# A macaron transformer layer on one core: zero rows by ScalarE, maxima split by VectorE, row loads and stack loads in another order

## The reference

```
quantise(W)  = clip(round(W / (mean|W| + 1e-5)), -1, 1)
ffn(u)       = relu(u @ quantise(W1).T + b1) @ quantise(W2).T + b2      # 128 -> 512 -> 128
attn(u)      = softmax(rope(q) @ rope(k).T / sqrt(8)) @ v, 16 heads of 8 channels, then @ Wo.T + bo
x = x + 0.5 * ffn(layernorm(x))
x = x + attn(layernorm(x))
x = x + 0.5 * ffn(layernorm(x))
```

## Time and profile before

| | us |
|---|---|
| median of 3 executions | 541.2 (540.09 to 543.0) |
| profiled execution, its time | 541.95 |
| profiled execution, span of the trace | 540.2 |
| TensorE busy | 498.2 (92%) |
| VectorE busy | 393.5 (73%) |
| ScalarE busy | 334.9 (62%) |
| GpSimd busy | 217.6 (40%) |
| mean granted clock of TensorE | 0.965 of full |

### The profile page before, as it was taken

How to read it: one execution, slowest core, us unless ns; L and a number is a source line. 1 busy time by engine, 2 the same in 40 slices (tenths; PEclk the granted TensorE clock), 3 DMA queues, 4 the chain that set the end, 5 groups by cost and what they waited for, 6 DMA issues and landing times.

```text
span 540.2 us, 8600 instructions
## 1 busy us (share of the span) xinstructions
PE 498.2 (92%) x3187; PEld 235.9 (44%) x3187; DVE 393.5 (73%) x579; ACT 334.9 (62%) x425; POOL 217.6 (40%) x292
## 2 busy tenths in 40 slices
PE   6686899989999989998999979999999999999986
PEld 3454434343453535352454533354435433443445
DVE  5672886957887678875787758877977898698124
ACT  2411346748857676765857655868686768577751
POOL 3403358434565183805552183418431831103202
PEclk7996889999999999998999998999999999999999
DMA  7859317402460139003360039013801480000000
GB/s 217 213 195 204 69 32 224 100 2 77 151 129 2 33 107 233 5 2 112 125 137 1 23 118 232 5 31 112 224 12 40 150 186 3 21 2 3 1 21 21
DMA packets 20681, 48.27 MB, mean 89 GB/s; under 512 B 2528, under 2 KB 5088, under 8 KB 19616
## 3 DMA queue, kind: packets, MB, share of 16 engines
q1 hardware_dynamic: 19328, 45.89, 32.0%
q10 hardware_dynamic: 1312, 1.84, 1.1%
HBM read 20.58 MB, written 18.87 MB: 73 GB/s over the span
## 4 chain that ended last, share of the span: by engine, by line
PE 62%; POOL 9%; DMA 8%; issue 7%; DVE 7%; ACT 5%; SPq 1%; POOLq 0%; ACTq 0%; DVEq 0%
PE heads_acc L575 17%; PE unit L558 11%; PE unit L539 11%; PE side L637 7%; DMA q_stack<-q_scratch 3%; DVE maxima L863 3%; PE side L631 3%; ACT probs L778 3%; PE side L617 2%; PE side L625 2%; PE side L613 2%; POOL normed_ffn L376 2%; DMA q_scratch<-q_parts 2%; DMA k_swap<-k 1%; PE heads_acc L645 1%
## 5 line engine op out<-in xcount | busy, mean ns | idle before, releaser
L863 DVE TENSOR_REDUCE maxima<-unit 128x2 f32<-128x1024 f32 x256 | 305.5, 1220 | 97.1 <-PE unit L539 96.1
L778 ACT ACTIVATE probs<-unit 128x1024 f32<-128x1024 f32 x256 | 256.6, 1027 | 112.1 <-PE unit L558 111.3
L575 PE MATMUL heads_acc<-probs,v_heads 128*32 128x512 f32 x1024 | 136.6, 611 | 1.3 <-ACT probs L778 1.1
L558 PE MATMUL unit<-q_stack,k_stack 64*128 64x512 f32 x512 | 119.9, 467 | 9.9 <-DMA q_stack<-max_T 5.7
L539 PE MATMUL unit<-k_stack,q_stack 62*128 62x512 f32 x512 | 115.3, 448 | 8.6 <-DMA q_stack<-q_scratch 5.7
L558 PEld LDWEIGHTS unit<-q_stack,k_stack 64*128 64x128 f32 x512 | 48.7, 187 | 79.4 <-issue 31.7
L539 PEld LDWEIGHTS unit<-k_stack,q_stack 62*128 62x128 f32 x512 | 49.7, 190 | 56.8 <-ACT probs L778 26.4
L1033 POOL TENSOR_SCALAR max_parts<-maxima 128x16 fp32r<-128x16 f32 x31 | 6.3, 205 | 129.5 <-DVE maxima L863 129.2
L637 PE MATMUL side<-w_q,hidden 128*128 128x128 f32 x416 | 57.2, 289 | 0.0
L637 PEld LDWEIGHTS side<-w_q,hidden 128*128 128x128 f32 x416 | 50.6, 197 | 13.6 <-issue 11.3
L575 PEld LDWEIGHTS heads_acc<-probs,v_heads 128*32 128x32 f32 x1024 | 21.0, 108 | 44.3 <-issue 36.1
(11 more groups left out here) (143 smaller groups left out, 443.5 us busy)
## 6 DMA issues: line engine op xcount, KB each, us to landing
k_scratch<-k_parts SPq DMA_DIRECT2D x16, 512.0 KB, 3.0
q_scratch<-q_parts SPq DMA_DIRECT2D x14, 512.0 KB, 2.8
k_stack<-k_scratch SPq DMA_DIRECT2D x14, 512.0 KB, 7.0
q_stack<-q_scratch SPq DMA_DIRECT2D x14, 512.0 KB, 9.4
resid<-in_x SPq DMA_DIRECT2D x8, 256.0 KB, 5.1
k_stack<-zero_rows SPq DMA_DIRECT2D x4, 480.0 KB
q_stack<-zero_rows SPq DMA_DIRECT2D x4, 480.0 KB
k_swap<-k SPq DMA_DIRECT2D x14, 128.0 KB, 2.3
```

Source lines behind the costliest of these rows:

```text
L558: mm = pe.matmul(to[:, e, :], k_stack[part, quad // NQ % 2, pair, kt * P:(kt + 1) * P], q_stack[part, quad // NQ % 2, pair, :], start=True ...
L575: mm = pe.matmul(heads_acc[32 * j:32 * j + 32, :], v_heads[:, b % 2, at, ODD * odd:ODD * odd + 32], probs[:, burst % RING, j, :], start=(k ...
L778: act.activation(probs[:, burst % RING, 2 * pp:2 * pp + 2, :], unit_of(PLACE["exp", n]), ACT.Exp, scale=SCALE).then_inc(s_exp, 1)
L863: dve.tensor_reduce(maxima[:, quad % 2, :, r], unit_of(PLACE["max", k]), AX_X, ALU.max).then_inc(s_max, 1)
```

## The change

1. **Zero rows.** The eight transfers of zeros (480 KB each) and the tile `zero_rows` go. ScalarE writes whole slots of a stack with `zeros(n, slot)`, one instruction each over 128x4096: slot 0 of k ahead of the prologue, slot 0 of q ahead of the transposition for the second batch, both slots 1 just ahead of `first_max_T`. The -1 rows are written per slot, after the zeros. New waits: SyncE for the zeros of k before the -1 rows, SyncE and ScalarE for the zeros of q before rows of q are loaded.
2. **First quad alone.** SyncE waits until the first quad's rows of q and k of batch 0 have landed before it issues the other three quads.
3. **Split on VectorE.** `split_max` and `split_first_max` move from GpSimd into `max_of` on VectorE, right behind the quad's last reduction (for quad 0, each pair's last).
4. **Order of SyncE.** `stack` of batch b + 1 is cut in two: the first quad (four transfers of 128 KB), then `max_row` of quad 2, then the other three quads (four of 384 KB). `max_row` of the next batch's quad 0 goes ahead of the swap of k. TensorE waits for the first quad and for the rest by semaphores of their own.
5. **Fills.** 10 instead of 4 ahead of the first m, 14 instead of 8 ahead of step 0, and 4 more in each of steps 0, 2 and 3, which wait for the copies of the first maxima.
6. **Steps.** `FIRST`, `STEADY` and `LATER` are written anew, with the same words in other steps.

```
-    "e m", "e m first_max_T1 attn_T@1", "e m m", "e m m k@1", ...
+    "e m fill1", "e m first_max_T1", "e m m fill2 attn_T@1", "e m m fill2 k@1", ...
-    ... "e m ffn1_up1 ffn1_stats@5", "e pv m ffn1_up2", "e m heads_T0 max_T3",
+    ... "e m max_T3 ffn1_stats@5", "e pv m ffn1_up1", "e m heads_T0 pv", "e m ffn1_up2 ffn1_up3", ...
...
-            sp.wait_ge(s_rows_fill, ROWS_FILLED[0])
             for e in range(2):
-                rows_to_stack(sp, "k", 0, e, slice(0, 2), s_stack_first)
+                rows_to_stack(sp, "k", 0, e, slice(0, 2), s_stack_first[0])
+            sp.wait_ge(*stacked(0, 0))
+            sp.wait_ge(s_zeros["q"], 1)
             stack(0, slice(2, NPAIR), s_stack[0])
-            zero_between(1)
+            minus_between(1)
...
                 if on("values", b):
-                    stack(b + 1, slice(0, NPAIR), s_stack[(b + 1) % 2])
+                    stack(b + 1, slice(0, 2), s_stack_first[(b + 1) % 2])
                 if 0 < b < B:
                     max_row(b * NQ + 2)
+                if on("values", b):
+                    stack(b + 1, slice(2, NPAIR), s_stack[(b + 1) % 2])
...
-                if on("proj", b):
-                    swap("k", b + 2)
                 if on("values", b):
                     max_row((b + 1) * NQ)
                 if on("proj", b):
+                    swap("k", b + 2)
                     swap("q", b + 2)
...
+            def zeros(n, slot):
+                tile = q_stack if n == "q" else k_stack
+                act.activation(tile[:, slot, :, :].rearrange("p h t -> p (h t)"), ones_f[:, 0:1].to_broadcast([P, NPAIR * S]),
+                               ACT.Copy, scale=0.0).then_inc(s_zeros[n], 1)
...
                 dve.tensor_reduce(maxima[:, quad % 2, :, r], unit_of(PLACE["max", k]), AX_X, ALU.max).then_inc(s_max, 1)
+                if quad == 0 and r % T == T - 1:
+                    split_first_max(r // T)
+                elif quad > 0 and r == QSTEPS - 1:
+                    split_max(quad)
...
+            def split_max(quad):
+                dve.wait_ge(s_max, (quad + 1) * QSTEPS)
+                wait(dve, s_maxT_psum, quad - 1)
+                whole = maxima[:, quad % 2, :, :]
+                dve.tensor_scalar(max_parts[:, :, 0, :], whole, 1.0, 0.0, ALU.mult, ALU.add).then_inc(s_split, 1)
+                dve.wait_ge(s_split, (quad - 1) * SPLIT_STEPS + 1)
+                dve.tensor_tensor(max_parts[:, :, 1, :], whole, max_parts[:, :, 0, :].bitcast(F32),
+                                  ALU.subtract).then_inc(s_split, 1)
```

More of the change, by code:

```diff
@@ L44 @@
 STACK_LANDED = 16 * 4
[L46 removed]
+ROWS_FILLED = 16 * 2
 ROPE_STEPS = 5
@@ L235, in macaron_layer @@
         s_row_values = sem("stack_row_values_set")
-        s_rows_fill = sem("stack_rows_filled")
+        s_rows_fill = [sem(f"stack_rows_filled_{k}") for k in ("even", "odd")]
+        s_zeros = {n: sem(f"{n}_stack_slots_set_to_zero") for n in "qk"}
         s_v_fill = sem("v_heads_filled_with_constants")
@@ L354, in stacked @@
         def stacked(j, g):
-            return (s_stack_first, STACK_LANDED) if j == 0 and g == 0 else (s_stack[j % 2], (j // 2 + 1) * STACK_LANDED)
+            return (s_stack_first if g == 0 else s_stack)[j % 2], (j // 2 + 1) * STACK_LANDED
         last = B - 1
@@ L417, in load_x @@
                 sp.dma_start(batch_rows(j), x[j].rearrange("(p t) d -> p t d", t=T)).then_inc(s_x[j], 16)
-            def zero_between(slot):
-                for tile in (k_stack, q_stack):
-                    for e in range(2):
-                        to = tile[TILE_ROWS * e + PROD:TILE_ROWS * e + ROWS_MAX, slot, :, :].bitcast(F32)
-                        sp.dma_start(to, zero_rows[:].unsqueeze(1).to_broadcast([ROWS_MAX - PROD, NPAIR, S])).then_inc(s_rows_fill, 16)
             load_x(0)
@@ L439, in _, with minus_between @@
             load_x(2)
-            sp.wait_ge(s_row_values, 2)
-            for e in range(2):
-                to = k_stack[TILE_ROWS * e + ROWS_MAX:TILE_ROWS * (e + 1), :, :, :].bitcast(F32).rearrange("p b h t -> p (b h) t")
-                sp.dma_start(to, minus_rows[:].unsqueeze(1).to_broadcast([PARTS, 2 * NPAIR, S])).then_inc(s_rows_fill, 16)
-            zero_between(0)
             for j in range(3, B):
                 load_x(j)
+            def minus_between(slot):
+                sp.wait_ge(s_zeros["k"], slot + 1)
+                for e in range(2):
+                    to = k_stack[TILE_ROWS * e + ROWS_MAX:TILE_ROWS * (e + 1), slot, :, :].bitcast(F32)
+                    sp.dma_start(to, minus_rows[:].unsqueeze(1).to_broadcast([PARTS, NPAIR, S])).then_inc(s_rows_fill[slot], 16)
+            sp.wait_ge(s_row_values, 1)
+            minus_between(0)
             def swap(n, j):
@@ L691, in _ @@
                         burst += 1
+                    elif use[0] == "fill":
+                        pe.wait_ge(s_first_maxT, use[1])
+                        fill(FILL_BESIDE_EXP)
                     else:
@@ L793, in _ @@
             act.wait_ge(s_b1, 16)
+            act.wait_ge(s_ones, 1)
+            zeros("k", 0)
             for use in PROLOGUE:
                 name, part, j, _ = use
+                if use[:3] == ("ffn1_T", 0, 1):
+                    zeros("q", 0)
                 if name in ("q_first", "k_first"):
@@ L811, in _ @@
             act.wait_ge(s_const, 16 * FIRST_CONST_DMAS)
+            zeros("k", 1)
+            zeros("q", 1)
             side_part(("first_max_T", 0, 0, HEADS_BANK))
@@ L818, in _ @@
                         take_heads(use[2] * 2 + use[1])
+                    elif use[0] == "fill":
+                        continue
                     else:
@@ L852, in ln_stats, with split_first_max @@
                     dve.bn_aggr(mean_var[n][:, t, :], stats[n][:, t, :]).then_inc(s_var[n], 1)
+            def split_first_max(p):
+                dve.wait_ge(s_max, (p + 1) * T)
+                whole = maxima[:, 0, :, p * T:(p + 1) * T]
+                dve.tensor_scalar(first_parts[:, p, :, 0, :], whole, 1.0, 0.0, ALU.mult, ALU.add).then_inc(s_first_split, 1)
+                dve.wait_ge(s_first_split, p * SPLIT_STEPS + 1)
+                dve.tensor_tensor(first_parts[:, p, :, 1, :], whole, first_parts[:, p, :, 0, :].bitcast(F32),
+                                  ALU.subtract).then_inc(s_first_split, 1)
+            def split_max(quad):
[6 more added lines that the diff above has]
+                                  ALU.subtract).then_inc(s_split, 1)
             def max_of(k):
```

47 lines of the change are left out of this document (11 added, 36 removed), and 34 rows, old and new, of tables (FIRST, LATER, STEADY).

## The result

The changed kernel takes 527.0 us (median of four executions, 526.6 to 527.6), the kernel before, run with it, 540.7 (540.1 to 543.0). The ratio is 0.974, 95% interval 0.971 to 0.977. The profiled execution has a span of 524.9 us and a mean granted clock of 0.99, against 540.2 and 0.965.

The account below looks back on a forecast made before the run. TensorE was taken as all but full in the loop, leaving its waits, half clock and the opening to win. 3.8 + 2.3 + 1.5 + 0 + 1.5 + 5.7 + 5.4 - 7 = 13.2 off 541.2 gives 528 us, range 516 to 540.

Parts of the forecast that it names:

- First quad's rows: Opening: q's first quad lands in 3.3 us once SyncE holds the large transfers; gain 3.8 us, bounds 0 and 4.3.
- Zeros on ScalarE: Opening: four ScalarE instructions of 3.6 us each replace the zero transfers and fit in its idle time; cost 0.
- Batch 0's second half: Waits of 0.9 for q's rows and 1.3 behind `heads_T0` go, 0.7 between `ffn1_up2` and `ffn1_up3` comes; gain 1.5 us.
- Ends of batches and clock: Batch ends: waits for rows of maxima go, gain 5.7 us; half clock in batches 3 and 4 goes, gain 5.4 us.
- The splits: Batches 1 to 7: VectorE pairs of 0.97 us, lengthened by chance meetings with GpSimd; a quarter reaches TensorE, cost 7 us.
- GpSimd's split: Batch 4: TensorE's 1.6 us wait for this split goes, the lower bound of the 5.4 us clock gain.
- Stack in two pieces: The fourth wait for a row of maxima, 0.8 us behind 2 MB of stack rows, goes; only 512 KB lie before it.
- Steps placed anew: New order of steps on each engine, same products: 0, within 2 us either way.
- hidden pairs: Rival: VectorE's split pairs are hidden and cost 1 us instead of 7; 522 us, chance 0.20.
- VectorE becomes the bound: Slower case: splits held by GpSimd delay reductions, all 33 pairs at 0.97 us reach the end; 553 us, chance 0.11.
- Clock stays: Rival: half clock comes from thin work in general, so 2.3, 1.5 and 3.8 us are lost; 528 + 7.6 = 536, chance 0.14.
- another wait: Rival: at batch ends TensorE waits for the exponential or the bank instead, 5.7 us lost; 534 us, chance 0.10.

Follow-up runs that it names:

- two experiments: The swap of k put ahead of the next batch's row again in the changed kernel, 539.0 us; all splits on VectorE alone in the kernel before, 547.6 us.
- the best experiment: Changed kernel with quad 1's split on GpSimd in batches 1, 4, 5 and 6 alone, the other splits on VectorE: 520.7 us, ratio 0.962.
- partial versions: Kernel before with the next batch's row ahead of the swap of k, 549.3 us; with all splits on VectorE, 547.6 us; with both, 548.5 us.
- the version with the row ahead of the swap: Kernel before with one edit, the next batch's row of maxima issued ahead of the swap of k: 549.3 us, ratio 1.012.
- the swap ahead: Changed kernel with the swap of k ahead of the next batch's row of maxima again: 539.0 us, ratio 0.994.
- the fills of before: Changed kernel with 4 fills ahead of the first m, 8 ahead of step 0 and none in steps 0, 2 and 3: 528.0 us, ratio 0.978.
- no hold: Changed kernel without SyncE's wait for the first quad ahead of the three larger quads: 535.5 us, ratio 0.989.
- rows behind the stack: Changed kernel with the row of quad 2 issued behind all eight stack transfers instead of between the two pieces: 548.1 us, ratio 1.015.
- zeros by transfers: Changed kernel with zero rows written by eight 480 KB transfers again, without ScalarE's four instructions, x of batches 3 to 7 loaded behind the first slot's zeros: 539.0 us.

## Why the prediction was right, and where its steps were not

The forecast was 528.0 us with 516 to 540; measured 527.0. It held in its sum, and the table of stages shows the waits that it named gone. That the sum is so close is in part luck. By the spans the gain is 15.3 where 13.2 was forecast: the opening to step 7 came out 2.2 us better, batches 1 to 4 3.8 better and batch 7 1.7 better, the rest of batch 0 1.7 worse and batches 5 and 6 3.9 worse. Taken one by one:

- *First quad's rows, 3.8.* Measured 5.2, outside its upper bound of 4.3. The last transfer of q takes 2.5 us instead of 7.06, not the 3.3 taken, and not the 2.8 of k that I used as the bound: that is 4.6. The other 0.6 is that it starts at 39.08 instead of 39.69, which no term had. The first m still waits 1.17.
- *Eight maxima, 2.3.* Measured 2.5, clock 1.00 in place of 0.50.
- *Steps 0 to 7, 1.5.* Measured 2.1, with VectorE busy 17.53 of 18.00: the idle time of VectorE was the bound, and nearly all of it was used.
- *Zeros on ScalarE, 3.6 us each and cost 0.* 3.63, and 0.93 us of cover left in place of 1.6. This part was right. "No cost" was also what I said of the transfers they replace, and there the step failed: 12 us. I looked at what waits for those transfers today, and found nothing; I didn't ask what would stand behind them when the first row is issued 7 us sooner. The other waits of the opening had hidden it.
- *Batch 0's second half, 1.5.* Measured -0.2. The two old waits (0.9 and 1.3) went as said, but 0.99 came behind `ffn1_up2` in place of 0.7, and 0.44, 0.45 and 0.20 for two reductions and a bank.
- *Ends of batches and clock, 5.7 and 5.4.* 10.1 came in batches 1 to 4, against 10.3 without the splits' share. The rows are early as forecast, batch 3 is as long as batch 2 (58.1 and 58.2) and batch 4 takes the 52.6 of a `LATER` batch. That the clock fell because of the waits at the ends isn't shown: in the traces of two experiments three such waits each were followed by full clock. For batch 4 the prediction also read the rows wrongly: its half clock began at 321.5 in the kernel before, 1.5 us behind the wait for GpSimd's split (ended at 320.01) and 8 us behind the batch's start. What is shown is that without waits no half clock is left in batches 1 to 4 of the trace.
- *The splits, -7 between 1 and 27.* The held pairs cost 6.3 us (the run with quad 1 moved in four batches). The size was right, but its path was other than I worked it out. A mean pair takes 0.28 + 0.33 = 0.61 us, not 0.97, and it isn't chance: of the 28 pairs of batches 1 to 7 three take 2.0 to 2.5 us (batches 1, 5 and 6), each of them quad 1's, which falls 4 us behind the start of its batch beside `xb_out` and `rope`. The other pairs of batches 1 to 7 take at most 0.65. A mean over chance meetings doesn't point to that place; which GpSimd instructions run there, the trace of before could have told. The share of GpSimd that went into that mean was also misread: by the earlier trace rows it is 41 to 50%, with batch 3 the lowest, not 45 to 50.
- *GpSimd's split, 1.6 as a part of the clock term.* The largest mistake of size, in the gain. On the trace of before, 1.9 us of TensorE's waits named it. With the splits on GpSimd in their soonest places the changed kernel loses 16. What I wrote of it, "nothing on the path waits for it except the split", failed there: TensorE waits 14.5 us for layer norms of GpSimd, some 9 of them by the order that I chose in that run. The price of the move in the old order stays open.
- *Stack in two pieces, 0.8 within the 5.7.* Worth 22, as the maxima now come while the stack transfers are on their way.
- *Steps placed anew, 0 within 2.* Worth 5 to 6, by the bank behind `heads_T0` in batches after 0.

Of the rivals: hidden pairs (522) would be nearly the time of the best experiment, 520.7, which is the changed kernel without its held pairs; they were not hidden. That VectorE becomes the bound is what batch 5 shows for one quad: a held pair of 2.5 us, then a wait of 1.74. Over all pairs the mean is 0.61 us, but most pairs reach no one's path. "Clock stays" and "another wait" at batch ends didn't happen.

The terms that were sized from waits in the trace before add up to the measured time. As prices of the single edits they are wrong. Undoing seven parts one at a time costs 16, 22, 12, 11, 8, 6 and (by the times) 2 us, 77 in all, where the change gives 14. Doing one or two alone in the kernel before costs 5 to 8 us instead of gaining. I read both as one structure: TensorE is full, and each of these waits lies a little behind the one before. Taking one away brings TensorE sooner to the next, which then costs about as much. The traces of the partial versions show new waits each time. Not all of them come from this, though: two of 2.5 us in the version with the row ahead of the swap come from the swap that the edit made late, and the 16 us contain an order of GpSimd's list that the kernel before did not have.

What stays open: why each of the three partial versions is slower than before and not only equal, and what decides whether half clock follows a wait. The kernel alone doesn't decide it: TensorE's wait of 1.7 us for the held pair of batch 5 is followed by half clock in three traces (the changed kernel, the swap ahead, the fills of before) and by none in three others (no hold, rows behind the stack, zeros by transfers). Nothing was tried against the remaining 1.17 us at the first m or the 0.99 in batch 0.

## What to carry to other kernels

When the full engine has several short waits, price an edit both in the old kernel and as one left out of the whole set: a part that gains nothing alone, or slows, can be one that the others need. For each transfer or small instruction that an edit makes earlier, list what stands ahead of it on its queue at the new time, not at the old one. When work goes from an in-order engine to another, count what stood queued behind its waits, and when you undo such a move to price it, put the work back into its old place in the queue. For the new engine look up which instructions of its neighbour run at just that place.

## What the runs showed of the hardware

- VectorE's small instructions from SBUF were held by two-input `tensor_tensor` instructions of GpSimd, and to their very end: 1.28 and 1.20 us in place of 0.175, both kinds of the pair. While GpSimd ran a `tensor_scalar` (L376, four in a row for 3.15 us), the split's `tensor_scalar` took 0.17 to 0.18 us (twice 0.28) and its `tensor_tensor` 0.17 to 0.38. Beside L398, a `tensor_scalar` of 0.62 us, one split instruction was held to its end in two of four meetings (0.63 and 0.47 us), and not in the other two. Three times VectorE's `tensor_tensor` began 0.02 us ahead of a two-input one of GpSimd (L400) and was not held (0.18 us), and once the `tensor_scalar` began 0.1 us before the end of one (L392, at 74.97) and took its usual 0.17. The Trainium skill, SBUF - State Buffer, section "Who interferes with whom", says that whoever issues first has the shared port pair for its whole instruction and blocks the other fully. Beside two-input instructions of GpSimd the trace agrees but for the meeting at 74.97; beside its `tensor_scalar` instructions it does so only in part.
- An 8 KB row issued 0.5 us behind the last of 2 MB on the same queue came into use 8.4 us after its issue, against 2.7 for one issued 0.6 us behind the last of 256 KB.
- In the traces half clock followed the 1.74 us wait of batch 5 in the changed kernel (but not the 1.73 us one of batch 6, nor the same wait of batch 5 in three other runs), the 5.0 us one of the opening without the hold and those of 2.7 to 3.1 us for the row of quad 2. It didn't follow six waits of 1.6 us in two experiments; in the kernel before it followed the same wait at batch 3 (half clock at 253.4, two microseconds behind it), not at batch 2.
